# A fused attention and expert kernel on one core: a place in SBUF for each of a layer's 31 output tiles, and row stores that wait for no later tile

## The reference, cut to what matters

```python
def _unipool_layer(xt, router, W1, W2):          # 2048 tokens, 16 experts
    logits = xt @ router
    probs = softmax(logits)
    w, idx = max(probs), argmax(probs)
    # for each expert i: where idx == i, add w * (silu(xt @ W1[i]) @ W2[i])
    return out
...
for router in routers:                           # 4 layers
    xt = _unipool_layer(xt, router, W1, W2)
x = x + attention(xn) + xt
xn = layernorm(x)
x = x + second_attention(xn) + one_of_8_experts(xn)
```

## Time and profile before

| | |
|---|---|
| median of 3 runs | 671.6 us (671.29 to 674.56) |
| span of the profiled execution | 669.4 us |
| busy: TensorE, VectorE, ScalarE, GpSimd | 591.2, 461.0, 423.6, 369.0 us |
| mean granted TensorE clock | 0.933 of full speed |
| first layer's first evacuation, last layer's last one | 65.2 us, 385.4 us |

### The profile page before, as it was taken

The page is one execution under the profiler, slowest core; times in us unless marked ns, Lnnn a source line. Parts: engine busy times, 40 slices in busy tenths (PEclk is TensorE's granted clock), DMA queues, the critical chain, the costliest instruction groups (busy, mean ns, idle before and its releaser), DMA issues.

```text
span 669.4 us, 14542 instructions
## 1 busy us (share of the span) xinstructions
PE 591.2 (88%) x4722; PEld 505.5 (76%) x4722; DVE 461.0 (69%) x1367; ACT 423.6 (63%) x1033; POOL 369.0 (55%) x395
## 2 busy tenths in 40 slices
PE   7879997789988899887999989999896687799996
PEld 7769987749978499885799965796674565668886
DVE  8633455664566655666542078989999999998946
ACT  3365554455555545563466647989988899987442
POOL 5461044540346402454255551278799999998974
PEclk9898998999999799986999989998897789989988
DMA  8953652116421155211443020000000000000002
GB/s 275 335 177 37 175 110 46 37 41 138 100 59 41 34 87 150 58 41 33 63 80 73 32 77 0 2 1 2 1 1 0 1 0 1 1 0 2 3 2 63
DMA packets 104123, 39.86 MB, mean 60 GB/s; under 512 B 85906, under 2 KB 96178, under 8 KB 103922
## 3 DMA queue, kind: packets, MB, share of 16 engines
q1 hardware_dynamic: 98018, 29.34, 19.6%
q0 software_dynamic: 4480, 9.30, 4.1%
q10 hardware_dynamic: 1552, 0.30, 0.2%
HBM read 20.32 MB, written 18.59 MB: 58 GB/s over the span
## 4 chain that ended last, share of the span: by engine, by line
PE 47%; POOL 18%; DVE 14%; issue 8%; ACT 5%; another core or an unknown queue 4%; DMA 2%; SPq 0%; ACTq 0%; POOLq 0%; DVEq 0%
PE PS L2396 18%; PE PS L2381 14%; POOL W1s L894 8%; POOL two_planes L812 4%; DVE W2s L1434 3%; PE PS L2296 2%; POOL wide L816 2%; PE PS L2325 1%; PE PS L2763 1%; PE PS L2287 1%; POOL two_planes L815 1%; ACT wide L1774 1%; PE PS L2780 1%; DMA sorted_x<-xrow,pos 1%
## 5 line engine op out<-in xcount | busy, mean ns | idle before, releaser
L776 POOL DMA_INDIRECT sorted_x<-xrow,pos x93 | 90.3, 971 | 173.0 <-DVE pos L1249 87.3
L2396 PE MATMUL PS<-W2s,wide 128*128 x992 | 146.9, 293 | 22.9 <-ACT wide L1774 12.3
L2396 PEld LDWEIGHTS PS<-W2s,wide 128*128 128x128 f32 x992 | 131.6, 197 | 27.0 <-issue 26.3
L2381 PE MATMUL PS<-wide,swt 128*128 128x128 f32 x992 | 133.6, 279 | 0.9 <-DVE wide L1314 0.9
L2381 PEld LDWEIGHTS PS<-wide,swt 128*128 128x128 f32 x992 | 122.6, 194 | 1.3 <-DVE swt L1308 1.3
L1774 ACT ACTIVATE wide<-PS 128x512 f32<-128x512 f32 x124 | 73.3, 591 | 65.2 <-PE PS L2381 37.6
L1782 ACT ACTIVATE xrow<-PS,tags 128x144 f32<-128x144 f32 (+1 forms) x124 | 46.7, 376 | 58.8 <-PE PS L2396 45.8
L894 POOL TENSOR_TENSOR W1s<-W1s,kT 128x1024 f32<-128x1024 f32 x21 | 50.0, 2385 | 8.2 <-DVE W1s L1581 7.0
L1994 ACT ACTIVATE W1s<-W1s,ab 128x128 f32<-128x128 f32 x168 | 51.4, 401 | 4.5 <-DVE W1s L1581 4.3
L1308 DVE COPY swt<-W1s 128x512 f32 x64 | 27.4, 430 | 37.0 <-PE PS L2381 27.8
L1317 DVE STREAM_TRANSPOSE wide<-wide 128x128 f32<-128x128 f32 x116 | 33.4, 300 | 28.0 <-DMA wide<-sorted_x 27.3
(11 more groups left out here) (434 smaller groups left out, 1320.9 us busy)
## 6 DMA issues: line engine op xcount, KB each, us to landing
wide<-sorted_x SPq DMA_DIRECT2D x224, 32.0 KB
sorted_x<-wide SPq DMA_DIRECT2D x9, 520.0 KB, 3.3
W1s<-in_L_ffn_W_dram SPq DMA_DIRECT2D x1, 4096.0 KB
sorted_x<-wide SPq DMA_DIRECT2D x1, 2015.0 KB, 12.1
sorted_x<-xrow,pos POOLq DMA_INDIRECT x109, 2.8
sorted_x<-wide SPq DMA_DIRECT2D x3, 455.0 KB, 2.9
xres<-in_L_attn_x_dram SPq DMA_DIRECT2D x4, 256.0 KB, 4.8
xrow<-results SPq DMA_DIRECT2D x4, 256.0 KB, 4.1
```

The source lines that it names most:

```text
L776: pool.indirect_dma_start(xs_dram[l + 1][:, :], bass.IndirectOffsetOnAxis(ap=pos[:, t:t + 1], axis=0), xrow[:, t % NR, 0:XW], None).then_i ...
L2381: m = pe.matmul(PS[:, 2 + n, f * P:(f + 1) * P], w1st[:, (c - 1) % WB, f * P:(f + 1) * P], xring[:, (c - 1) % R, :], start=True, stop=True)
L2396: m = pe.matmul(PS[:, 4 + n, 0:w], hTs[:, n, f * P:(f + 1) * P], W2s[:, f * YW:f * YW + (E - 1) * NF + w][:, bass.ds(w2, w)], start=(f == ...
```

## The change

`xrow` gets NS = 31 places, so that each tile of a layer has its own. ScalarE's wait on `y_put` goes. The 16 semaphores become one, since SyncE's waits at a layer's start and end of the loop need only the sum. The wait on `y_ev` ahead of the stores of the first three groups (`PACE`) goes too. To find the memory, `kT` becomes a view of the last 2048 numbers of `xrow` in each partition, behind the 16 places that the second block uses, and the small integer tables `row_i` and `rev_i` move into `wide`.

```diff
-    PACE = (10, 9, 8)
...
+    assert NT * YW + N <= NS * YW
...
-        xrow = sb("xrow", [P, NT, YW])
-        xcur = xrow[:, :, 0:D]
+        xrow = sb("xrow", [P, NS, YW])
+        xrow_f = xrow[:, :, :].rearrange("p t d -> p (t d)")
+        xcur = xrow[:, 0:NT, 0:D]
...
-        kT = sb("kT", [P, N])
+        kT = xrow_f[:, NS * YW - N:NS * YW]
...
-        row_i = sb("row_i", [P, NS], I32)
-        rev_i = sb("rev_i", [P, E], I32)
...
+        row_i = hbuf[:, S:S + NS].bitcast(I32)
+        rev_i = hbuf[:, S + NS:S + NS + E].bitcast(I32)
...
-        y_put = [sem(f"y_put{r}") for r in range(NR)]
+        y_put = sem("y_put")
...
-                    for r in range(NR):
-                        sp.wait_ge(y_put[r], 16 * PUTS[r] * l)
+                    sp.wait_ge(y_put, 16 * NS * l)
...
                     for t in range(*GROUPS[g]):
-                        if g < len(PACE):
-                            pool.wait_ge(y_ev, l * NS + min(NS, t + PACE[g]))
                         pool.indirect_dma_start(xs_dram[l + 1][:, :], bass.IndirectOffsetOnAxis(ap=pos[:, t:t + 1], axis=0),
-                                                xrow[:, t % NR, 0:XW], None).then_inc(y_put[t % NR], 16)
+                                                xrow[:, t, 0:XW], None).then_inc(y_put, 16)
...
-                    if t >= NR:
-                        act.wait_ge(y_put[t % NR], put_through(l, t - NR))
                     w = YW if l < L - 1 else D
                     act.wait_ge(tags_ready, 2 * l + (1 if t < R else 2))
-                    act.activation(xrow[:, t % NR, 0:w], PS[:, 4 + c % 2, 0:w], ACT.Copy,
+                    act.activation(xrow[:, t, 0:w], PS[:, 4 + c % 2, 0:w], ACT.Copy,
```

More of the change, by code:

```diff
@@ L321, in build @@
         Kc = qT[:, :].rearrange("p (t h i) -> p t h i", t=C, h=HP)
-        Qc = kT[:, :].rearrange("p (t h i) -> p t h i", t=C, h=HP)
+        Qc = kT.rearrange("p (t h i) -> p t h i", t=C, h=HP)
         Vc = vtok[:, :, :].rearrange("p t d -> p (t d)").rearrange("p (t h i) -> p t h i", t=C, h=HP)
         bKc = wdec[:, :, :].rearrange("p b (t h i) -> p (b t) h i", h=HP, i=HD)
-        xcur_f = xrow[:, :, :].rearrange("p t d -> p (t d)")[:, 0:XN]
+        xcur_f = xrow_f[:, 0:XN]
         X = [v.rearrange("p (c h i) -> p c h i", h=HP, i=HD) for v in (xcur_f, u[0][:, 0:XN], u[0][:, XN:2 * XN])]
@@ L350, in build @@
         vT = u[7].rearrange("p (b t) -> p b t", b=B)
-        vsq = kT[:, :].rearrange("p (b t) -> p b t", b=B)
+        vsq = kT.rearrange("p (b t) -> p b t", b=B)
         vstd, vinv = mx, first
@@ L510, in build @@
         SLOT_USES = [[c for c in PAIR_AT if c // 2 % RP == r] for r in range(RP)]
-        PUTS = [(NS - r + NR - 1) // NR for r in range(NR)]
         def pair_loaded(l, c):
@@ L671, in _ @@
                             matrix_part(1)
-            for r in range(NR):
-                sp.wait_ge(y_put[r], 16 * PUTS[r] * L)
+            sp.wait_ge(y_put, 16 * NS * L)
             for g in range(NG):
@@ L708, in _ @@
             step(pool.iota(row_i[:, 0:NT], pattern=[[P, NT]], base=0, channel_multiplier=1))
-            step(pool.tensor_copy(xrow[:, :, D], row_i[:, 0:NT]))
+            step(pool.tensor_copy(xrow[:, 0:NT, D], row_i[:, 0:NT]))
             step(pool.memset(ones_bf[:, :], 1.0))
@@ L1162, in choose @@
                 dve.wait_ge(y_ev, l * NS + GROUPS[g][1])
-                lg = xrow[:, tt, D:YW]
+                lg = xrow[:, GROUPS[g][0]:GROUPS[g][1], D:YW]
                 step(dve.tensor_reduce(mx[:, tt], lg, AX_X, ALU.max))
@@ L1186, in weigh @@
                 step(dve.reciprocal(ex[:, tt, :], ex[:, tt, :]))
-                mark(dve.tensor_reduce(xrow[:, tt, D + 1], ex[:, tt, :], AX_X, ALU.add))
-                mark(dve.tensor_copy(xrow[:, tt, D], tags[:, GROUPS[g][0]:GROUPS[g][1], 0]))
+                own = slice(*GROUPS[g])
+                mark(dve.tensor_reduce(xrow[:, own, D + 1], ex[:, tt, :], AX_X, ALU.add))
+                mark(dve.tensor_copy(xrow[:, own, D], tags[:, own, 0]))
             def weigh_last(l):
                 i, tt = NFG + (l + 1) * NGR - 1, group_slots(NGR - 1)
-                mark(dve.tensor_copy(xrow[:, tt, D], tags[:, GROUPS[NGR - 1][0]:NS, 0]))
+                own = slice(*GROUPS[NGR - 1])
+                mark(dve.tensor_copy(xrow[:, own, D], tags[:, own, 0]))
                 dve.wait_ge(exp_done, i + 1)
                 step(dve.tensor_reduce(esum[:, tt], ex[:, tt, :], AX_X, ALU.add))
-                return mark(dve.tensor_scalar(xrow[:, tt, D + 1], esum[:, tt], float(E), 0.5, ALU.add, ALU.mult))
+                return mark(dve.tensor_scalar(xrow[:, own, D + 1], esum[:, tt], float(E), 0.5, ALU.add, ALU.mult))
             def rooms(l, g):
```

4 lines of the change are left out of this document (1 added, 3 removed).

## The result

The changed kernel takes 695.44 us (median of 4 runs, 693.67 to 697.12) where the kernel before takes 672.33 (4 runs, 671.29 to 674.56). The ratio is **1.037**, 95% interval 1.033 to 1.041: slower, by 23 us. The forecast was 684.6 us, range 666 to 694. The direction was right, the size was not, and the median lies just above the range. In the ratios of this text the runs more than 1.5% above the fastest of the same kernel are left out, in the medians none is.

What follows compares the result with a forecast made beforehand. Prediction: stretches with stores lose time because back-to-back stores hold TensorE's news; the ring's wait never binds. Layers lose 4.8 + 4.8 + 3.5, about 13 us: 669.4 + 13 = 682.4, plus 2.2 median offset gives 684.6 us, range 666 to 694.

Steps and rivals of the forecast that it cites:

- The ring's wait: ScalarE's wait for an earlier store before reusing a place: said never to bind, so removing it is worth 0.
- hold TensorE's news: Back-to-back GpSimd stores delay word that TensorE has finished, by 1.43 to 1.45 us a store; a lone store does not.
- The fixed price per store: Rival: each store costs the same however spaced, so joining runs costs 0 us; 671.5 us, chance 0.18.
- the leak: Rival: fewer runs, and a long one lets two tiles out within an eight; -5.7 us, 665.9 us, chance 0.20.
- The rule of separate ports: Skill page: engine and DMA ports are disjoint and TensorE's side never waits, so run length costs nothing; sum about 0.
- Group 0, 3.9 us a layer: A layer's first eight stores go in one run instead of four, three and one: 3.9 us later, bounds 0 and 5.8.
- Two tiles behind, 2 x 1.87 + 0.2: After the first eight stores, tile 14 comes out when tile 16 did before, at 1.87 us a tile: 3.9 us.
- Group 1, 2.8 us a layer: Next eight stores in one run instead of five and three single: tile 22 comes out 2.8 us later.
- bound of 4.2: Upper bound for the second eight stores: tile 21, not 22, comes out at the run's end, 4.2 us later.
- 3.5 us for the whole first layer: First layer's total loss, against 4.8 in the others, because nothing was released within its run of five stores.
- Groups 2 and 3, a gain of 1.9 us a layer: Later stores as two separate fours instead of three and six: gain 1.9 us; bounds gain 5.1, loss 2.
- Its upper case: Rival that nothing gets out during a run: 8.1 us a layer, 24 in three, 696 us; no chance given.

Runs made afterwards that it cites:

- the pace (12, 9, 8): Kernel before with each store of the first eight-store group waiting for two more evacuations than under (10, 9, 8): 659.32 us, ratio 0.990, where before took 665.14.
- The run made to test it: Kernel before with only the pace of group 2 taken away, on a chip with holds: 672.77 us, ratio 1.004, where before took 671.53.

## Why the prediction was right, and where it failed

**The ring's wait never binds: right.** The 31 places are worth nothing, in either direction (ratio 1.003 with the pace put back). The mechanism was right too: runs of back-to-back stores hold TensorE's news, and the pace was what kept the runs short. Both eights came where they were forecast, and behind group 0's the held tile came out after 11.7 to 12.1 us, forecast 11.44. The fixed price per store fell with the pace (12, 9, 8); the leak fell too, since besides tile 12 only tile 13 came out within each group 0, as forecast. The rule of separate ports, put beside the fixed price, gave the wrong time. But no run shows TensorE waiting at a port: in the first layer it stood idle for 5.09 us, its matmuls done, while ScalarE and VectorE waited to hear of it.

**Group 0, 3.9 us a layer: too small, and the step that failed.** "Two tiles behind, 2 x 1.87 + 0.2" takes it that the tiles behind the hold come out at full speed. In the changed kernel, counted from the first store, tile 16 is evacuated after 18.24, 14.98 and 16.44 us in the three layers, before after 11.42, 11.26 and 11.43: later by 6.8, 3.7 and 5.0. The middle one looks like the forecast, in part by luck: tile 15 came out 0.75 us behind tile 14, which made up for the slow matmuls behind it. To tile 19 the stretch grew by 7.2, 5.3 and 5.4 us, 17.9 in all against 11.7.

What was left out is that TensorE, idle in the hold, went on at a granted clock of 0.50 to 0.56 where it had 1.00 before. Eight matmuls took 2.28 us in place of 1.24, and stretches with equal counts of matmuls differ as the clock does. No run changed the clock alone. An estimate from the rows of the changed kernel: TensorE's busy time in the three stretches from tile 14 to 16 (5.94, 2.32, 4.73 us), times the share of the clock that was missing, is 3.0, 1.2 and 2.1 us. The forecast fell short by 3.3, 1.4 and 1.5.

**Group 1, 2.8 us a layer: the place right, the size near, another tile.** The forecast had tile 21 out midway and tile 22 released at the end. In all three layers tile 20, which before came out 1.3 to 1.4 us after the first store, came out after 2.1 to 4.3 us, and tile 21 was the one released, after 11.7, 11.5 and 10.1 us: the case that the forecast had as its bound of 4.2. The part from tile 19 to 24 grew by 2.6, 4.3 and 1.9 us, 8.8 in all. The forecast comes to 7.1, since its 3.5 us for the whole first layer leave 1.5 for group 1. The reason given for that, that nothing was released within the first layer's run of five, doesn't tell the layers apart: in both tile 20 came out 1.4 us after the run's start and nothing more until tile 21 at its end. The first layer lost the most, 7.9 us.

**Groups 2 and 3, a gain of 1.9 us a layer: not shown.** In the changed kernel the two fours are there and the last part did shrink, by 1.9 and 2.2 us, and then grew by 0.2, so 3.8 of the forecast 5.7. But the change with its pace, which has no such fours, has a short last part too (14.9 against 16.3), and so have the kernels that lost only group 0's or group 1's pace (14.8 each): single executions differ by as much as the term. The run made to test it didn't have the fours. Whether they gain anything stays open.

**The sum.** The span grew by 25.7 us, forecast 13. Of the 12.7 that are missing group 0 has 6.2, group 1 1.7, groups 2 and 3 1.9, and the last layer and the rest, put at 0, have 2.9.

**The range.** Its upper case, 5.8 + 4.2 - 1.9 a layer or 696 us, was nearly the result. For group 1 it had the right tile. For group 0 it had no tile 13 out of the eight, and tile 13 did come out; what made up its cost was the half clock. There the number is right for another reason.

## What to carry to other kernels

Ahead of loosening a wait in a stream of indirect stores, look at what the wait spaces: here the wait that seemed to idle GpSimd for 28.5 us was worth 23 to 24 us. The best setting found, (12, 9, 8), puts an evacuation between nearly all stores of group 0. Doing the same to groups 1 and 2 pushed nine stores into one run at the layer's end, and the gain was gone. A stall is to be costed with what follows it: TensorE came out of these holds at half clock, which added an estimated 1 to 3 us a time. And a kernel whose time differs by 8% between chips is to be tuned and judged on the kind that shows the effect, with a run of the kernel before beside it each time.

## What the runs showed of the hardware

- The hold was seen on some chips only. The kernel before took 665.1, 667.3, 669.4, 671.5 and 672.3 us in five comparisons, and 622.9 and 623.1 on two other chips. On the second of these the change was worth 1.000, and in its second layer a tile came out every 1.87 us through eight stores in a row.
- Where it exists, it is 1.43 to 1.44 us for each indirect store of a run of ten to twelve, the same for 128 rows, 32 rows and an eighth of the bytes, and 1.43 for a run of seven. Behind the eights of the changed kernel the held tile came out 10.1 to 12.1 us after the first store. Issuing one takes 0.97 us (0.86 with 32 rows) and 0.30 between. Eight fixed-address stores of GpSimd on the same queue took 4.69 us together and held nothing.
- With 0.63 us or more between nearly all of them, eight stores cost nothing that the evacuations show. Two pairs 0.47 us apart held like four in a row.
- From tile 14 to tile 16, behind group 0's run of eight, the granted clock was 0.50 to 0.66 in eight places and 0.91 and 0.92 in two, in four kernels. Eight matmuls took 2.28 us at the lower of its two levels, 1.2 GHz, and 1.24 at the upper. What decides between the places stays open, as does what in the chips makes the hold.
- Whether the pace (12, 9, 8) is neutral on the chips without the hold wasn't tried.
